# The softmax's division in a patch attention with three convolutions: on ScalarE, patch by patch, in place of VectorE

## The reference

```python
stk = _neighborhood(x)                      # [B,H,W,9,C], zero padded
mask = _neighborhood(ones)[..., 0]
q = einsum('bhwd,de->bhwe', x, Q_P)
k = einsum('bhwkd,de->bhwke', stk, K_P)
v = einsum('bhwkd,de->bhwke', stk, V_P)
scores = einsum('bhwke,bhwe->bhwk', k, q) * mask
alpha = softmax(scores, axis=-1)
t = x + einsum('bhwk,bhwke->bhwe', alpha, v)
t_in = t
t = relu(conv(t, ff1_kernel) + ff1_bias)    # 64 -> 64
t = relu(conv(t, ff2_kernel) + ff2_bias)    # 64 -> 128
t = relu(conv(t, ff3_kernel) + ff3_bias)    # 128 -> 64
return t_in + t
```

## Time and profile before

| | |
|---|---|
| median of 3 runs | 2083.73 us (2083.67 to 2085.44) |
| the profiled execution, its own time | 2084.2 us |
| its span | 2082.4 us |
| PE / DVE / ACT busy | 97% / 87% / 52% of the span |
| chain that ended last | PE 96%, DVE 2%, ACT 1%, issue 1% |
| granted clock of PE, whole span | 0.992 of full speed |

### The profile page before, as it was taken

The page is one execution under the profiler, slowest core; times in us unless marked ns, Lnnn a source line. Parts: engine busy times, 40 slices in busy tenths (PEclk is TensorE's granted clock), DMA queues, the critical chain, the costliest instruction groups (busy, mean ns, idle before and its releaser), DMA issues.

```text
span 2082.4 us, 61988 instructions
## 1 busy us (share of the span) xinstructions
PE 2025.3 (97%) x23866; PEld 1240.9 (60%) x23866; DVE 1815.4 (87%) x2502; ACT 1088.4 (52%) x3086; POOL 17.2 (1%) x28
## 2 busy tenths in 40 slices
PE   4899999999999999999999999999999999999997
PEld 3566656656665655655656655665656665665554
DVE  3699899899899899899889899899888989989986
ACT  3464555555555555555555455455455455455422
POOL 3000000000000000000000000000000000000000
PEclk9899999999999999999999999999999999999999
DMA  5555555555555555555555554554555555554532
GB/s 146 124 149 170 164 143 171 156 148 167 155 152 167 155 157 158 157 163 150 160 158 155 161 168 141 165 167 140 166 165 141 170 162 144 168 166 144 155 128 86
DMA packets 286054, 320.89 MB, mean 154 GB/s; under 512 B 87802, under 2 KB 220218, under 8 KB 279482
## 3 DMA queue, kind: packets, MB, share of 16 engines
q1 hardware_dynamic: 285982, 319.92, 53.0%
HBM read 150.23 MB, written 33.82 MB: 88 GB/s over the span
## 4 chain that ended last, share of the span: by engine, by line
PE 96%; DVE 2%; ACT 1%; issue 1%; DMA 0%; SPq 0%; DVEq 0%; ACTq 0%
PE conv_banks L502 32%; PE conv_banks L462 16%; PE conv_banks L527 13%; PE side_banks L527 13%; PE side_banks L443 6%; PE side_banks L422 4%; PE conv_banks L402 4%; PE side_banks L431 3%; PE side_banks L453 3%; PE side_banks L414 2%; ACT prob L724 1%; DMA xs<-x_bands 0%; DVE work L962 0%; DVE deven L882 0%; DVE deven L883 0%
## 5 line engine op out<-in xcount | busy, mean ns | idle before, releaser
L502 PE MATMUL conv_banks<-dodd,w3f 128*64 128x512 f32 (+2 forms) x1616 | 491.4, 581 | 11.0 <-DVE work L929 9.3
L502 PE MATMUL conv_banks<-deven,w3f 128*64 128x512 f32 (+2 forms) x1616 | 490.3, 579 | 0.0
L724 ACT ACTIVATE prob<-side_banks,negmax 128x100 f32<-128x100 f32 x1024 | 344.9, 378 | 162.5 <-DVE negmax L847 162.5
L462 PE MATMUL conv_banks<-dt,w1f 128*64 128x256 f32 (+2 forms) x4128 | 377.6, 378 | 0.0
L462 PEld LDWEIGHTS conv_banks<-dt,w1f 128*64 128x64 f32 (+1 forms) x4128 | 233.7, 135 | 121.0 <-issue 42.1
L502 PEld LDWEIGHTS conv_banks<-dodd,w3f 128*64 128x64 f32 x1616 | 148.3, 137 | 245.4 <-issue 219.7
L724 ACT ACTIVATION_READ_ACCUMULATOR prob<-side_banks,negmax 128x1 f32 x1024 | 246.9, 241 | 0.0
L502 PEld LDWEIGHTS conv_banks<-deven,w3f 128*64 128x64 f32 x1616 | 152.8, 137 | 143.1 <-issue 139.7
L736 ACT COPY rq<-conv_banks 128x512 f32<-128x512 f32 x128 | 68.7, 589 | 305.2 <-PE conv_banks L402 305.2
L962 DVE TENSOR_TENSOR work<-side_banks,work 128x1024 f32<-128x1024 f32 (+1 forms) x130 | 154.4, 1230 | 78.6 <-PE side_banks L527 78.6
L741 ACT COPY probt<-side_banks 100x1024 f32<-100x1024 f32 x128 | 130.2, 1017 | 157.2 <-PE side_banks L431 157.2
(11 more groups left out here) (92 smaller groups left out, 3282.5 us busy)
## 6 DMA issues: line engine op xcount, KB each, us to landing
xk<-x_keys SPq DMA_DIRECT2D x65, 800.0 KB
xc<-x_bands SPq DMA_DIRECT2D x65, 650.0 KB, 4.8
xr<-x_bands SPq DMA_DIRECT2D x260, 128.0 KB, 2.9
dodd<-dodd SPq DMA_DIRECT2D x65, 512.0 KB, 5.6
out<-work SPq DMA_DIRECT2D x64, 512.0 KB, 4.1
xs<-x_bands SPq DMA_DIRECT2D x130, 128.0 KB, 3.1
dt<-dt SPq DMA_DIRECT2D x65, 256.0 KB, 4.8
deven<-deven SPq DMA_DIRECT2D x65, 256.0 KB, 6.1
```

The source lines that it names most:

```text
L462: mm = nc.tensor.matmul(bank[(LOWER, UPPER)[o], n * 256 + lo * 64:n * 256 + hi * 64], w1f[i][rows, m, s, o * C:o * C + C], dt[rows, lo + s ...
L502: mm = nc.tensor.matmul(bank[rows, lo_ * 128:hi_ * 128], w3f[:, m, s, odd * C:odd * C + C], source[:, lo_ + s // 2:hi_ + s // 2, m], start ...
L724: last = nc.scalar.activation(prob[:, g, a], score_banks[g // 2][:, g % 2, a * KEYS:(a + 1) * KEYS], ACT.Exp, bias=negmax[:, g, a:a + 1], ...
```

## The change

`scale` leaves DVE, where only its reciprocal stays, under the name `invert`. ACT gets a `scale` of its own: for each of the 8 tiles of a half it multiplies `prob`, 128x100, in place by the tile's column of reciprocals. `prob_ready` is now given by ACT. In the loop the first half stands after the last exponentials and before `keep_y`, the second half after `keep_y` and before the second part of `u_high`. Ahead of the loop both halves stand between the exponentials and `keep_turned`.

```diff
+            def scale(b, half):
+                act.wait_ge(inv_done, b * 2 + (half + 1))
+                for g in (2 * half, 2 * half + 1):
+                    for a in range(GROUP):
+                        last = nc.scalar.mul(prob[:, g, a], prob[:, g, a], expinv[:, g, a:a + 1])
+                last.then_inc(prob_ready, 1)
...
                 for g in range(GROUPS):
                     exps(b, g)
                 for half in range(2):
+                    scale(b, half)
+                for half in range(2):
                     keep_turned(b, half)
...
                 if att == ASK:
                     exps(b + 2, 3)
+                    scale(b + 2, 0)
                 if att >= MIX:
                     keep_y(b + 1, 0)
                     keep_y(b + 1, 1)
+                if att == ASK:
+                    scale(b + 2, 1)
                 u_high(G, k, 1)
...
-            def scale(b, half):
+            def invert(b, half):
                 groups = slice(2 * half, 2 * half + 2)
                 dve.wait_ge(exp_done, b * GROUPS + (2 * half + 2))
                 nc.vector.reciprocal(expinv[:, groups], expsum[:, groups]).then_inc(inv_done, 1)
-                dve.wait_ge(inv_done, b * 2 + (half + 1))
-                p = prob[:, groups].rearrange("q g a n -> q (g a) n")
-                inv = expinv[:, groups].rearrange("q g (a o) -> q (g a) o", o=1).broadcast_to([128, HALF, KEYS])
-                nc.vector.tensor_tensor(p, p, inv, ALU.mult).then_inc(prob_ready, 1)
...
                 middle(G, k, CONV3)
                 if att == ASK:
-                    scale(b + 2, 0)
+                    invert(b + 2, 0)
                 u_low(G, k, 0)
                 if att == ASK:
-                    scale(b + 2, 1)
+                    invert(b + 2, 1)
                 outer3(G, k)
```

More of the change, by code:

```diff
@@ L983, in attend @@
                 for half in range(2):
-                    scale(b, half)
+                    invert(b, half)
             attend(0)
```

## The result

The changed kernel takes 2172.84 us (median of 4 runs, 2172.36 to 2174.02) against 2084.53 for the one before (4 runs, 2083.67 to 2085.44). The ratio is 1.0425, 95% interval 1.0408 to 1.0441. That is 88 us slower; 2176 was forecast. The profiled execution has a span of 2171.0 us, 88.6 more than the span before.

The account below looks back on a forecast made before the run. PE bounds the kernel, DVE close behind. 53 ordinary steps x 1.25 = 66.3, 8 special steps 16.8 and 9.0 ahead of the loop make 92 us, so 2176 us; range 2128 to 2230.

Parts of the forecast that it names:

- The base: Loop step of 31.00 us set by PE; removing DVE's covered products is worth nothing there.
- The spacing p: Time between starts of successive ACT multiplications, taken as 0.28 us, bounds 0.23 and 0.32.
- ReLU row: Profile row of two ACT ReLUs with per-partition operand; gives 0.85 ns per element and a spacing of 0.26 us.
- The rival without overlap: ACT multiplications each cost their whole duration, 378 ns: 2.81 us a step, 2276 us; chance 0.04.
- (a): Before conv3's fourth tile's last two taps, PE awaits y copies and prob's first half: 1.15 us idle a step.
- y pair: ACT's two back-to-back copies of the mixed values y, taken as 1.17 us, behind the first eight multiplications.
- (c): Before conv2's last group, PE waits until DVE has read the EVEN banks: 0.1 us more a step.
- The special steps: First and second loop steps of each image pair, 8 in all, priced at 2.1 us each: 16.8 us.
- Ahead of the loop: Three attentions before the loop, where nothing hides ACT: 3.2, 3.2 and 2.6 us later, 9.0 together.
- Not slower: Rival: ACT's block fits PE's room before the taps and DVE's relief ends waits; 2072 to 2084 us, chance 0.05.
- Lower clock: Rival: new waits drop TensorE to 1.2 GHz, some 2.3 us a step more, 2315 us; chance 0.03.
- What I had told the reader to look for: PE idle 1.1 us before the taps, step 32.2 to 32.3, DVE idle about 3 before second low part, busy 128 less.

Follow-up runs that it names:

- E1: Kernel before with the division left out on both engines, DVE keeping the reciprocals: 2083.48 us, ratio 0.9995.
- E6: Changed kernel with ACT's multiplications taking only 20 of the 100 keys, the other 80 left undivided: 2120.47 us, ratio 1.0170.
- E7: Changed kernel with both y copies made by DVE in the loop, and DVE dividing ahead of the loop: 2106.02 us, ratio 1.0102.
- E8: Changed kernel with PE's wait for DVE's EVEN reads moved behind the three other waits at the same place: 2162.36 us, ratio 1.0378.
- E4: Changed kernel in the loop, but DVE products in the three attentions ahead of it: 2164.64 us, ratio 1.0386.
- E5: Changed kernel with the second cast of u ahead of the second block of multiplications: 2182.65 us, ratio 1.0477.
- E10: Changed kernel with both y copies ahead of both blocks of multiplications: 2197.44 us, ratio 1.0549.
- E3: Changed kernel with only the second half on ACT in the loop; first half and everything ahead of the loop DVE products: 2087.25 us, ratio 1.0014.
- E2: Changed kernel with only the first half on ACT in the loop; second half and everything ahead of the loop DVE products: 2149.88 us, ratio 1.0321.
- E9: Kernel before with 16 more multiplications of 128x100 on ACT at the end of each loop step: 2086.14 us, ratio 1.0008.

## Why the prediction was right

The mechanism was the one forecast, and 2176 was 3 us high. Point by point:

- *The base.* PE sets the step, and the products on DVE were covered. E1 shows it: 31.00 with them gone.
- *The spacing p.* 0.28 taken, 0.267 measured, between the bounds 0.23 and 0.32 and beside the ReLU row's 0.26. E6 gives the same slope of 0.82 ns as that row's 0.85. The rival without overlap falls: a multiplication lasts 449 ns in the mean and they start 0.267 apart.
- *The wait at (a).* 1.15 us forecast, 0.93 measured. Of the 0.22, 0.10 is p (8 x 0.013) and 0.05 the y pair (1.12 against 1.17); the last 0.07 is room at the taps that I had read too small: the weights come 1.30 us later than before for 0.93 lost, so the first 0.37 is harmless, where I took 0.30 (E7's 0.35 at no cost agrees).
- *The wait at (c).* 0.1 forecast, 0.31 measured. This term was mis-sized, in the other direction. (Its own sum is a little off too: 1026.84 + 7.08 is 1033.92, not 1033.95.) I counted DVE's chain against PE's point of asking with no time for the handover; the trace shows 0.24 us from DVE's end to PE's weights, and E8 shows that three quarters of it goes when the late wait stands behind the other three. The two errors cancel to 1.25 against 1.27, so the good sum for an ordinary step is partly luck.
- *The special steps.* 8 x 2.1 = 16.8 forecast, 12.5 measured. The first step of a pair has more room than the second, 1.40 against 1.82; I priced both like the second, and that one 0.3 too high.
- *Ahead of the loop.* 9.0 forecast, 8.6 in the profiled execution, and E4 gives 8.2 back in the medians. The profiles of E5, E8 and E10 with 5.8 to 6.2 show that this term also moves with the execution by more than its error.
- *Not slower.* It needed p of 0.14 or less at (a), and DVE's relief to end waits. PE's waits for L937 (L929 before) are what they were, 9.4 us from 100 us on. E3 shows what that rival would have looked like: with only the second block on ACT the loop step is 31.00.
- *Lower clock.* In the loop the granted clock stayed 1.00 through steps with these waits (both stretches of the step at 1017.5 and 1036.2 us). The span's mean was 0.986 instead of 0.992, and the difference stands in the first 90 us. The change isn't shown to be its cause: other executions of the kernel before had 0.987 to 0.992, those of the changed one 0.986 to 0.991.
- *What I had told the reader to look for.* PE idles at (a), but by 0.93 and not 1.1. DVE's idle time is where I did not put it: 4.12 us ahead of the outer sums of conv3, ended by PE's tile, and only 0.55 ahead of the second low part, ended by the cast. The step of 32.27, the release by the y copy, and DVE's 126 us less came as said.

## What to carry to other kernels

Moving work from a busy engine to one that idles half the time costs what it delays on the path between the two nearest points where the bounding engine asks. Here eight multiplications cost 1.0 us a step in front of the y copies (E2), eight behind them nothing (E3), and sixteen nothing at the step's end (E9). The costs don't add up from single places: both blocks of eight together cost 1.27, since the second meets less room once the first has pushed it back. Read the room at each such point from the timeline, ask for the work's spacing and not its duration, and where an in-order engine makes several waits in a row, put the one that comes last at the end.

## What the runs showed of the hardware that I had not expected

- The order of PE's waits in a row can cost time. At (c), with the late wait first of four, PE's weights came 0.24 us after the release; with it last, 0.06. That was worth 10.5 us over the run. It isn't a fixed price for each wait: at (a), where the late one stands first of two, it was 0.05 in the changed kernel and 0.12 in E2 and E4. What in the three further waits at (c) takes the time isn't shown.
- A float32 ACTIVATE with a per-partition factor has a fixed part of 0.185 us in its spacing, by an estimate from two sizes (0.201 at 20 elements and 0.267 at 100). Its recorded duration, 0.41 to 0.56 us for 100 elements, says little about that.
- The clock level ahead of the loop differs between executions of the same code. From 30 to 40 us the granted clock was 0.50 of full speed, the lower level, in the changed kernel's profile and 1.00 in those of E5 and E10, whose code there is the same. The loop started at 77.99 in the first and at 75.5 in the other two, and the first 32 matmuls of conv1 took 4.62 us and 3.5 (before the change 3.85). One profile of each kernel can't tell what the change did there. The chain of the changed kernel, then that of E5:

```profile
79.98 4.62 PE conv_banks L462 x32
```

```profile
75.51 1.98 PE conv_banks L402 x8
77.50 3.50 PE conv_banks L462 x32
```
